# Cross-attention of layer 1: straight-line code, group products in the keys' and values' PSUM bank, both transposes of a batch in a row

## What is computed

```python
def _L1_xattn_ref(query, key, value, Wq, bq, Wk, bk, Wv, bv, Wo, bo):
    H, D = (16, 8)
    q = (query @ Wq.T + bq).reshape(B, Sq, H, D)
    k = (key @ Wk.T + bk).reshape(B, Sk, H, D)
    v = (value @ Wv.T + bv).reshape(B, Sk, H, D)
    scores = jnp.einsum('bqhd,bkhd->bhqk', q, k) / np.sqrt(D).astype(jnp.float32)
    attn = jax.nn.softmax(scores, axis=-1)
    out = jnp.einsum('bhqk,bkhd->bqhd', attn, v).reshape(B, Sq, E)
    return out @ Wo.T + bo
...
    x = x + _L1_xattn_ref(_layernorm(x, axis=-1), ctx_1024, ctx_1024, ...)
```

## Time and profile before

| | us |
|---|---|
| time, median of 3 runs | 1570.16 |
| time, lowest and highest | 1567.33 to 1570.26 |
| span of the profiled execution | 1628.3 |
| cross-attention of layer 1 within it, about | 566 to 1080 |
| one group of four batches in the loop | 15.52 |

### The profile page before, as it was taken

How to read it: one execution, slowest core, us unless ns; L and a number is a source line. 1 busy time by engine, 2 the same in 40 slices (tenths; PEclk the granted TensorE clock), 3 DMA queues, 4 the chain that set the end, 5 groups by cost and what they waited for, 6 DMA issues and landing times. The chain is left out here.

```text
span 1628.3 us, 45122 instructions
## 1 busy us (share of the span) xinstructions
PE 1396.8 (86%) x14710; PEld 1044.0 (64%) x14710; DVE 1078.7 (66%) x3440; ACT 813.7 (50%) x2400; POOL 694.3 (43%) x1302
## 2 busy tenths in 40 slices
PE   3888888868877699999999999969999999957773
PEld 2666666645756566666666666647777777746672
DVE  3899899846212178878878888746777777862224
ACT  2565565522132267777777777734344443413330
POOL 2455555520454334444444444421224443364553
PEclk9999999979799789999999999979999999977887
DMA  6555533110010212122121221200000000013224
GB/s 196 166 188 186 187 131 116 59 53 13 22 32 24 93 60 72 62 72 75 59 75 59 75 72 62 69 3 1 1 4 14 13 11 12 14 37 82 77 72 162
DMA packets 78364, 113.04 MB, mean 69 GB/s; under 512 B 12480, under 2 KB 55753, under 8 KB 78160
## 3 DMA queue, kind: packets, MB, share of 16 engines
q1 hardware_dynamic: 70352, 97.93, 18.6%
q0 software_dynamic: 6784, 12.06, 2.4%
q10 hardware_dynamic: 1152, 2.10, 0.3%
HBM read 78.95 MB, written 35.00 MB: 70 GB/s over the span
## 5 line engine op out<-in xcount | busy, mean ns | idle before, releaser
L1812 ACT ACTIVATE c_pr<-c_pS,c_nm 128x257 f32<-128x257 f32 x512 | 238.5, 472 | 103.4 <-DVE c_nm L1948 103.4
L1948 DVE TENSOR_REDUCE c_nm<-c_pS 128x1 f32<-128x257 f32 (+1 forms) x384 | 173.2, 505 | 42.9 <-PE c_pS L1692 42.9
L2279 ACT ACTIVATE s_k<-s_pK 128x512 f32<-128x512 f32 x128 | 76.4, 597 | 182.8 <-PE s_pK L2176 181.3
L1696 PE MATMUL c_pT<-cst,c_pr 128*128 128x128 f32 x1024 | 157.4, 276 | 0.1
L2176 PEld LDWEIGHTS s_pK<-s_hT,AH 128*128 128x128 f32 x1024 | 126.7, 198 | 22.1 <-ACT s_k L2279 18.2
L2176 PE MATMUL s_pK<-s_hT,AH 128*128 128x128 f32 x1024 | 140.4, 288 | 0.5 <-ACT s_hT L2274 0.5
L1696 PEld LDWEIGHTS c_pT<-cst,c_pr 128*128 128x128 f32 x1024 | 117.4, 142 | 13.2 <-issue 12.9
L2197 PE MATMUL s_pM<-BH,s_uT 128*128 128x128 f32 x1024 | 123.3, 280 | 1.4 <-DVE LG L2431 1.4
L2197 PEld LDWEIGHTS s_pM<-BH,s_uT 128*128 128x128 f32 x1024 | 120.4, 197 | 1.8 <-DVE LG L2431 1.8
L1692 PE MATMUL c_pS<-c_ks,c_qq 32*128 32x257 f32 x1024 | 92.7, 431 | 14.3 <-issue 9.8
L1525 POOL DMA_INDIRECT rows_out<-f_yb,f_token_of x78 | 76.1, 976 | 63.3 <-DVE f_token_of L1538 41.4
(11 more groups left out here) (371 smaller groups left out, 3397.2 us busy)
## 6 DMA issues: line engine op xcount, KB each, us to landing
rows_in<-c_blank SPq DMA_DIRECT2D x32, 520.0 KB, 2.9
a_ctxT<-in_ctxT SPq DMA_DIRECT2D x32, 514.0 KB, 3.7
c_ctxT<-in_ctxT SPq DMA_DIRECT2D x128, 128.5 KB
a_ctxN<-in_ctxR SPq DMA_DIRECT2D x32, 512.0 KB, 4.2
f_hb<-rows_in SPq DMA_DIRECT2D x39, 130.0 KB
f_w<-in_f_w SPq DMA_DIRECT2D x16, 256.0 KB, 3.4
a_ctxL<-in_ctxL SPq DMA_DIRECT2D x128, 16.0 KB, 3.6
f_w<-in_f_w SPq DMA_DIRECT2D x16, 128.0 KB, 3.3
```

Of the source, the lines that this page charges most:

```text
L1696: mm = pe.transpose(pT[:, c, j, :], pr[:, b % 2, j, c * P:(c + 1) * P], k("ident"))
L1812: act.activation(pr[:, b % 2, c, :], pS[:, c, 0:S], ACT.Exp, bias=nm[:, c:c + 1], accum_out=den[:, b % 2, c:c + 1]).then_inc(e_ready.sem, 1)
L1948: dve.tensor_reduce(nm[:, c:end], pS[:, c:end, 0:S], AX.X, ALU.max, negate=True).then_inc(max_ready.sem, 1)
L2279: act.activation(k2[:, c * HK:(c + 1) * HK, :], pK[:, c % 2, :, :], ACT.Copy).then_inc(k_ready.sem, 1)
```

## The change

1. The `Fori` loops of all five engines become Python loops: every group is written out, and every wait is on a constant.
2. The two turns of a batch stand together, and nothing stands between them.
3. The group products move from `pS` to columns 384 to 511 of `pM` (`pP`). In that bank they must keep clear of ACT's read of the keys and DVE's read of the values. Norm, queries and the projection stand ahead of `keys`, behind a wait for the values (`v_ready`); last keys (now b=2) and scales (now b=3) stand behind `sums`, ahead of `values`, behind a wait for `k_ready`. The waits for a product's reader move with them.
4. Scores of a head group wait only for the exponential of the same head group of the batch before.
5. The projection of group g-1 is now done in group g+1 (b=0), and DVE's `add_output` with it, behind a new wait for ACT's copy of keys n+2 (`k_ready`). In the last group `add_output` of the group before moves to the tail, ahead of DVE's `gather`.
6. The norm's statistics and power move to b=3, for the group after the next; only the scaling (L225) stays in b=0. POOL's `scales` moves to b=2 and `rinv` gets two buffers. ACT's copies of norm and queries stand behind its copy of the keys.

```diff
-            def group_product(b, g, n, first, last):
-                pe.wait_ge(e_ready.sem, e_ready.at(n, 1 if b != 2 or first else 2))
-                if b == 0 and not first:
-                    last_keys(g - 1)
...
+            def heads_product(g, b, n):
+                if b == 2:
+                    pe.wait_ge(k_ready.sem, k_ready.at(n + 1))
+                    last_keys(g - 1, pP)
...
+            def group_product(g, b, n):
+                pe.wait_ge(v_ready.sem, v_ready.at(n + 1))
+                if b == 0 and g > 1:
+                    project(g - 2, pP)
+                if b == 1 and g + 1 < G:
+                    norm_T(g + 1, pP)
+                if b == 2 and g + 1 < G:
+                    queries(g + 1, pP)
...
             def scores(b, n):
...
-                pe.wait_ge(e_ready.sem, e_ready.at(n - 1))
                 for c in range(NQ):
+                    pe.wait_ge(e_ready.sem, e_ready.at(n - 1, c + 1))
...
-            def body(g, first, last):
+            def body(g):
...
+                    product_read(g, b)
+                    if g > 0:
+                        heads_product(g, b, n)
+                    if n + 1 < B:
                         values((b + 1) % BG, n + 1)
-                    if turns:
+                    if n > 0:
                         turn((b - 1) % BG, n - 1, 0)
-                    group_product(b, g, n, first, last)
-                    if turns:
                         turn((b - 1) % BG, n - 1, 1)
-                    if b < BG - 2 or not last:
+                    if n + 2 < B:
+                        if g > 0:
+                            heads_product_read(g, b)
+                        group_product(g, b, n)
                         keys(g if b < BG - 2 else g + 1, (b + 2) % BG, n + 2)
-                    group_product_read(b, g, first, last)
...
-            body(0, True, False)
-            with pe.Fori(1, G - 1) as g:
-                body(g, False, False)
-            body(G - 1, False, True)
+            for g in range(G):
+                body(g)
...
# DVE
+                    if b == 0 and g > 1:
+                        dve.wait_ge(k_ready.sem, k_ready.at(n + 2))
+                        add_output(g - 2, pP)
+                    if b == 0 and g + 1 < G:
                         n4.vector_scale(dve, x_of(g + 1), g + 1)
...
+                    if b == BG - 1 and g + 2 < G:
+                        n4.vector_stats(dve, x_of(g + 2), g + 2)
```

More of the change, by code:

```diff
@@ L1664, in _, with norm_T, queries @@
             pe.sem_inc(v_done.sem, v_done.credit)
-            def norm_T(g):
+            def norm_T(g, out):
                 pe.wait_ge(n4.h_ready.sem, n4.h_ready.at(g))
-                pe.transpose(pG[0], n4.h[:, :], k("ident")).then_inc(hT_done.sem, 1)
-            def queries(g):
+                pe.transpose(out, n4.h[:, :], k("ident")).then_inc(hT_done.sem, 1)
+            def queries(g, out):
                 pe.wait_ge(hT_ready.sem, hT_ready.at(g))
-                pe.matmul(pG[0], w("wq1"), hT[:, :], start=True, stop=True).then_inc(q_done.sem, 1)
+                pe.matmul(out, w("wq1"), hT[:, :], start=True, stop=True).then_inc(q_done.sem, 1)
             def keys(g, b, n):
                 pe.wait_ge(ctx_loaded[b].sem, ctx_loaded[b].at(g))
-                if not (isinstance(n, int) and n == 0):
+                if n > 0:
                     pe.wait_ge(v_ready.sem, v_ready.at(n - 1))
@@ L1721, in project @@
+            def project(g, out):
                 pe.wait_ge(on_ready.sem, on_ready.at(g))
-                pe.matmul(pG[0], on[:, :], w("wo1"), start=True, stop=True).then_inc(y_done.sem, 1)
-            def group_product(b, g, n, first, last):
-                pe.wait_ge(e_ready.sem, e_ready.at(n, 1 if b != 2 or first else 2))
-                if b == 0 and not first:
-                    last_keys(g - 1)
-                if b == 1 and not last:
-                    norm_T(g + 1)
-                if b == 2:
[L1732 to L1737, removed]
@@ L1754, in body @@
+            def group_product(g, b, n):
[4 more added lines that the diff above has]
+                    norm_T(g + 1, pP)
+                if b == 2 and g + 1 < G:
+                    queries(g + 1, pP)
+            def body(g):
+                last = g + 1 == G
                 for b in range(BG):
                     n = g * BG + b
-                    turns = not first or b > 0
@@ L1757, in body @@
                     scores(b, n)
-                    if not first or b > 1:
-                        if b == 2 and not first:
+                    if n > 1:
+                        if b == 2 and g > 0:
                             pe.wait_ge(om_ready.sem, om_ready.at(g - 1))
                         sums((b - 2) % BG, n - 2)
-                    if b < BG - 1 or not last:
+                    product_read(g, b)
+                    if g > 0:
+                        heads_product(g, b, n)
+                    if n + 1 < B:
@@ L1832, in body @@
                     exps(b, n)
-                    if b == 1 and not last:
-                        normed(g + 1)
-                    if b == 2 and not last:
-                        queries(g + 1)
-                    if not first or b > 0:
+                    if n > 0:
                         turned((b - 1) % BG, n - 1)
-                    if b < BG - 2 or not last:
+                    if n + 2 < B:
                         keys((b + 2) % BG, n + 2)
-            normed(0)
+                    if b == 1 and g + 1 < G:
+                        normed(g + 1, pP)
+                    if b == 2 and g + 1 < G:
+                        queries(g + 1, pP)
+            normed(0, pG[0])
             act.wait_ge(bqs_ready.sem, 1)
-            queries(0)
+            queries(0, pG[0])
             keys(0, 0)
             keys(1, 1)
-            body(0, True, False)
-            with act.Fori(1, G - 1) as g:
-                body(g, False, False)
-            body(G - 1, False, True)
+            for g in range(G):
+                body(g)
             turned(BG - 1, B - 1)
@@ L1861, in spread @@
                 pool.wait_ge(q_ready.sem, q_ready.at(g))
-                if not (isinstance(n, int) and n < 2):
+                if n > 1:
                     pool.wait_ge(s_done.sem, s_done.at(n - 2))
@@ L1898, in add_bias @@
             def add_bias(g):
-                if not (isinstance(g, int) and g == 0):
+                if g > 0:
                     pool.wait_ge(x_ready.sem, x_ready.at(g - 1))
@@ L2026, in _ @@
             values(0, 0)
-            body(0, True, False)
+            body(0)
             dve.wait_ge(env["back_added"], NB - 1)
-            with dve.Fori(1, G - 1) as g:
-                body(g, False, False)
-            body(G - 1, False, True)
-            inverse_sums(BG - 1, B - 1, None)
-            last_keys(G - 1)
+            for g in range(1, G):
+                body(g)
+            inverse_sums(BG - 1, B - 1)
             turned(BG - 1, B - 1)
+            last_keys(G - 1, pG[0])
+            add_output(G - 2, pP)
             gather(G - 1)
-            scale(G - 1)
-            add_output(G - 1)
+            scale(G - 1, pG[1])
+            add_output(G - 1, pG[0])
 def self_layer1(env):
```

167 lines of the change are left out of this document (81 added, 86 removed).

## The result

| | before | after |
|---|---|---|
| time, median us | 1570.07 (1567.33 to 1570.26) | 1528.75 (1524.3 to 1533.7) |
| ratio, 95% interval | | 0.9737 [0.9714, 0.9761] |
| span of the profiled execution | 1628.3; again: 1568.8 | 1527.9 |
| cross-attention of layer 1, from its first instruction to self-attention's first | 515.7; again: 519.5 | 479.6 |
| of it up to the first scores | 10.5; 13.1 | 13.4 |

What follows compares the result with a forecast made beforehand. PE was taken to bound the kernel: 13.99 us of work a group plus waits of 0.45 and 0.10 gives 14.54 for 15.52. Net of the tail, 28 us less: 1542 us (forecast 1532 to 1552, range 1526 to 1560).

Steps and rivals of the forecast that it cites:

- rival 1: PE runs through, DVE's lateness is absorbed: group 14.0 to 14.2 us, 1523 to 1530 us; chance 12%.
- What bounds the kernel: Stage's loop group: only PE is near its length, busy 14.99 of 15.52 us.
- PE's work without waits: Per group, from distances between starts: four batches of 3.18 us plus products, 13.99 us.
- Loops: End of b=3: the branch costs PE 0.39 us a group, 29 times; other engines' branches priced at nothing.
- Batches: PE per batch after, without waits: b=0 3.40, b=1 3.29, b=2 3.76, b=3 3.54 us.
- L225: DVE's scaling in b=0: falls from median 1.09 to 0.35 us, since POOL's scales move to b=2.
- The scores' own wait is hidden: Next scores can start at 3.15 us, PE comes at 3.29 to 3.76: hidden by 0.1 us or more.
- The wait in b=1: PE, ahead of keys, waits 0.45 us for DVE's late values; bounds 0.2 to 0.9.
- The sum: Group 14.54 us, 0.98 less; 29.5 times gives 28.9, tail loses 1.0, net 28 us.
- Rival 2: L225 still meets a POOL step, or small waits add up: group 15.2, 1555 to 1565 us; chance 11%.
- Rival 3: Straight code is fetched slower than PE eats it: 1582 to 1620 us, taken as 1600; chance 7%.
- Rival 4: Ring of scores, maxima, exponentials sets the pace, freed time returns as waits: within 3 us of 1570; chance 6%.

Runs made afterwards that it cites:

- e6_order_only: The changed kernel with loops of two groups (groups 0, 1, 30, 31 straight) and waits on registers: 1544.0 us, ratio 0.9851 against the kernel before.
- e2_scale_first: The changed kernel with the norm's scaling (L225) ahead of `add_output` on DVE in b=0: 1525.71 us, ratio 0.9732 against the kernel before.
- b_again: The kernel before the change, unchanged, run once more for a second profile: 1570.56 us.
- e3_norm_back: The changed kernel with the norm's statistics and power back in b=0, POOL's `scales` behind them: 1540.23 us, ratio 0.9831 against the kernel before.
- e1_loops_only: The kernel before with its five loops written out and nothing else changed: 1555.3 us, ratio 0.9927 against the kernel before.
- e5_coarse_wait: The changed kernel with all four scores waiting for all four exponentials of the batch before: 1533.57 us, ratio 0.9777 against the kernel before.
- e8_turns_only: `e1_loops_only` with the second turn ahead of the group product, which stays in `pS`: 1556.81 us, ratio 0.9923 against the kernel before.
- e7_gather_first: `e2_scale_first` plus `gather(g - 1)` ahead of DVE's copy of the turned weights in b=1: 1522.48 us, ratio 0.9697 against the kernel before.
- e7_again: The kernel of `e7_gather_first`, unchanged, run once more: 1523.07 us, ratio 0.9709 against the kernel before.

## Why the prediction was right, and where not

The 1528.75 us lie in the stated range of 1526 to 1560, but not in the forecast itself (1532 to 1552, 64%). They lie where rival 1 stands (1523 to 1530, 12%), which the range took in. The mechanism held: what bounds the kernel, where it waits, and for whom. The sizes of the waits did not.

- **What bounds the kernel: right.** PE's stream sets the pace before and after.
- **PE's work without waits: the sum right, its terms in part by luck.** The count of 13.99 us, from start-to-start distances of before, was met at 13.98 once all waits were gone. But its terms were off and cancel. Scores, sums and a heads' product take 1.48 us (782.06 to 783.54, b=2) and 1.44 (b=3) for 1.58 each: 0.24 less, since the narrow product costs less where it follows the narrow sums. The queries take 0.33 for 0.22, the norm's transpose 0.15 for 0.11, and the keys of b=3 0.63 for 0.53: 0.25 more.
- **Loops: right for the kernel before.** 0.39 us a group predicted, 0.38 measured alone, so the other engines' branches are free there. The prediction also said that with less cover they would still cost only what PE's does. In the new order a loop costs 0.98 a pair of groups and not 0.39 (`e6_order_only`): that did not hold.
- **Batches: right but for b=1.** Predicted 3.40, 3.74, 3.76, 3.54; measured 3.39, 3.58, 3.76, 3.50. The change-over of 0.14 in b=0 went as read.
- **L225: right.** 1.09 to 0.34 us, because POOL has no step there. This is worth 0.37 us a group, since it stands on the only chain that PE waits for.
- **"The scores' own wait is hidden": nearly.** With one wait for all four a group is 0.11 longer.
- **The wait in b=1: right place, wrong size.** This is the term that was mis-sized. I predicted 0.45 there and 0.10 elsewhere; after has 14.23 - 13.98 = 0.25 in all, and `e2_scale_first` shows it as b=1's (3.58 to 3.33). By the steps, from the scores of b=0 at 775.08: `add_output` starts at 4.08 (I said 4.1); maxima at 4.54 (4.75); values end at 6.22 (6.4); PE is there at 6.04 (6.05) and goes on at 6.28. The 0.2 lie between `add_output` and the maxima. I summed durations, 0.29 + 0.35, where the starts in the trace stand 0.20 and 0.26 apart: DVE's records overlap as PE's do, and I had used distances for PE only. Of the 0.1 that I added for weights not loaded ahead, 0.06 came (6.22 to 6.28).
- **The sum.** 1.29 a group and not 0.98: 29.5 x 0.31 = 9.1 us more. The tail is 0.65 us shorter than in `b_again` where I had it 1.0 longer: 1.65 more; it is as short with the loops alone out, so the new order of the tail cost nothing. The middle lost 39.5 where 29.5 x 1.29 = 38.1. These 1.4 are no gain of the change that one could count on: they come from `b_again`'s long first group (17.77 us; 16.31 in the other profile). 28 + 9.1 + 1.65 + 1.4 = 40.2; up to the first scores after is 0.3 longer, and the stage shows 39.9.

Of the rivals, 1 is nearest to what happened, though PE does not run through: it waits 0.24. Its price does not follow from the prediction's own sum, by which groups of 14.0 to 14.2 give 1526 to 1532 us. Rival 2 fell with L225; `e3_norm_back` is what it looks like. Rival 3 fell: the straight code brings 82 packets for 41, and 28 of the 31 distances between groups are 14.22 or 14.23. Rival 4 fell: the freed time did not come back as waits, the kernel is 41 us faster and not within 3.

Where the 1.29 us of a group went: loops 0.38 (`e1_loops_only`). The other 0.91 can be read from PE's stream, as distances between starts in the written-out kernel before and in after (medians of 20 groups in the middle; sums and heads' product stand apart in the first and together in the second).

| us | `e1_loops_only` | after |
|---|---|---|
| both turns, b=0 | 1.02 | 0.87 |
| both turns, b=2 | 1.05 | 0.88 |
| turns, norm and keys, b=1, waits included | 2.17 | 1.81 |
| scores, sums and last keys | 1.58 | 1.48 |
| scores, sums and scales | 1.58 | 1.44 |
| queries | 0.42 | 0.33 |
| keys, b=3 | 0.53 | 0.63 |

So turns in one piece bring 0.32, the waits in b=1 0.36, the narrow products behind the narrow sums 0.24 and the queries 0.09, less 0.10 for the keys. The runs with one piece changed fit this without adding up to it, since they start from different kernels: L225 is worth 0.37 in after (`e3_norm_back`), the waits by head group 0.11 in after (`e5_coarse_wait`), the turns 0.16 in the bank of before (`e8_turns_only`). The new bank by itself was not measured.

## What to carry to other kernels

Count the bounding engine's work from the distances between starts, at the places in the trace where it does not wait: that sum is the size of what can be won and, as here, close to what an order without waits reaches. Count again where a new order changes a piece's neighbours. Cost a chain on the second engine in the same way, not by its durations. Where one step waits for another engine, put ahead of it whatever needs nothing of it, and look one batch further for the wait that comes up next.

## What the runs showed that I had not expected

- Straight code is nearly free here. In after, its repeats and every other written-out run with the norm's statistics in b=3, the fourth distance between groups is 0.23 to 0.35 us longer than the others (14.53 for 14.23; 14.28 for 13.98 in `e7_gather_first`). In after, DVE's aggregate of the norm starts 0.51 us late there, 0.16 elsewhere:

```profile
590.00 0.28 DVE L210 BATCH_NORM_STATS2 c_n_stats<-X 128x6 f32<-128x128 f32 x1
590.79 0.18 DVE L215 BATCH_NORM_AGGREGATE c_n_mv<-c_n_stats 128x2 f32<-128x6 f32 x1 [0.51 <-DVE c_n_stats L210]
```

  A packet of instructions on q14 moves in this stretch, but only from 591.48 us on, 0.7 us after the aggregate has started, and the written-out runs with the statistics in b=0 (`e1_loops_only`, `e3_norm_back`, `e8_turns_only`) bring a packet in that stretch too and show no such delay. The cause is open.
- The same edit that is worth 0.16 us a group in the stage with the old bank costs the kernel its whole gain with the new bank if left out (14.23 against 16.18 us).
- TensorE's granted clock is 0.50, the lower of its two levels, up to the first scores and rises in the first group. When it does is worth 2.3 us of this stage: 14.00 us at 0.92 in `e7_gather_first`, 16.30 at 0.72 in `e7_again`, with the same instructions.
